# A six-deep pipeline of a vision tower: the order lists of four engines laid out anew

## What is computed

```python
h = _L0_tok_ref(x, L0_tok_W, L0_tok_b)
h = jnp.concatenate([jnp.broadcast_to(cls_tok, (h.shape[0], 1, h.shape[2])), h], axis=1)
h = h + _L0_attn_ref(_layernorm(h, axis=-1), ...)   # 12 heads of 64, diagonal out, top 12 of 17 kept, softmax, w_out
h = h + _L0_ffn_ref(_layernorm(h, axis=-1), ...)    # ternary weights, int8-like activations, silu(gate) * up
h = h + _L1_attn_ref(_layernorm(h, axis=-1), ...)   # causal linear attention, 12 heads of 16, gated by an "interference"
h = h + _L1_ffn_ref(_layernorm(h, axis=-1), ...)    # relu, two projections, layernorm
return h
```

## Time and profile before

| | us |
|---|---|
| median of 3 runs | 718.96 |
| the runs | 718.26, 719.4, 718.96 |
| the profiled execution, device time | 718.05 |
| its span, first to last instruction | 716.2 |
| PE busy | 596.5 (83%) |
| VectorE busy | 534.0 (75%) |
| GpSimd busy | 349.6 (49%) |
| ScalarE busy | 255.5 (36%) |

### The profile page before, as it was taken

One profiled execution on the slowest core, in us unless ns is written; L12 is line 12 of the kernel. 1 busy time (PEld: TensorE's weight loads), 2 busy tenths in 40 slices (PEclk: granted clock), 3 DMA queues, 4 the chain that ended last, 5 costly groups with the idle time before them and its releaser, 6 DMA issues.

```text
span 716.2 us, 15345 instructions
## 1 busy us (share of the span) xinstructions
PE 596.5 (83%) x5065; PEld 484.1 (68%) x5065; DVE 534.0 (75%) x2149; ACT 255.5 (36%) x659; POOL 349.6 (49%) x884
## 2 busy tenths in 40 slices
PE   4277878998999999899999998999998998778562
PEld 3165566776777777677777767777776777666451
DVE  0715568789888988889897898989889888864432
ACT  2014143443525344353533435353443534232110
POOL 2020023665645566564655656465655645454432
PEclk9679999999999999999999999999999999765555
DMA  9710010000000000000000000000000000000000
GB/s 220 166 35 1 1 41 19 2 20 6 22 9 18 26 7 21 7 19 20 9 19 5 19 5 19 17 11 21 5 0 5 1 6 7 0 6 0 6 1 7
DMA packets 11122, 14.92 MB, mean 21 GB/s; under 512 B 2161, under 2 KB 8658, under 8 KB 11078
## 3 DMA queue, kind: packets, MB, share of 16 engines
q1 hardware_dynamic: 8774, 12.69, 7.1%
q10 hardware_dynamic: 2304, 1.67, 0.8%
HBM read 12.68 MB, written 1.67 MB: 20 GB/s over the span
## 4 chain that ended last, share of the span: by engine, by line
PE 62%; DVE 15%; ACT 7%; POOL 6%; issue 5%; SPq 4%; DMA 1%; POOLq 0%; DVEq 0%; ACTq 0%
PE bank_embed L1211 8%; PE bank_lin L1346 5%; PE bank_embed L1216 5%; PE bank_embed L1181 4%; PE bank_lin L1368 4%; PE bank_embed L1195 4%; PE bank_att L1285 4%; PE bank_lin L1087 3%; PE bank_lin L1336 3%; PE bank_embed L1087 3%; SPq L387 3%; POOL rstd_h L483 3%; PE bank_lin L1384 2%; PE bank_att L1275 2%; PE bank_embed L1199 2%
## 5 line engine op out<-in xcount | busy, mean ns | idle before, releaser
L1211 PE MATMUL bank_embed<-norm0T,w_qkv 128*128 128x119 f32 x456 | 61.3, 287 | 11.4 <-DMA g_out<-L_ffn_g_out 6.5
L482 POOL TENSOR_TENSOR spread<-moments,gain_eps 119x1 f32<-119x1 f32 x57 | 10.9, 192 | 120.2 <-DVE moments L674 120.2
L1211 PEld LDWEIGHTS bank_embed<-norm0T,w_qkv 128*128 128x128 f32 x456 | 57.4, 202 | 12.4 <-issue 6.6
L483 POOL TENSOR_TENSOR rstd<-spread,minus_half 119x1 f32<-119x1 f32 (+1 forms) x95 | 55.5, 585 | 7.4
L530 POOL TENSOR_TENSOR feat_k<-feat_qk,consts 96x238 f32<-96x238 f32 x38 | 23.2, 627 | 73.3 <-DVE feat_qk L834 73.3
L984 ACT COPY qkT<-bank_embed 128x357 f32<-128x357 f32 x76 | 31.1, 467 | 50.0 <-PE bank_embed L1216 50.0
L1368 PE MATMUL bank_lin<-feat_qk,feat_k 32*119 32x119 f32 x456 | 46.1, 294 | 1.6 <-DVE weightsT L743 1.3
L699 DVE TENSOR_REDUCE scores<-bank_att 119x51 f32<-119x357 f32 x76 | 36.6, 522 | 14.3 <-PE bank_att L1245 13.2
L1368 PEld LDWEIGHTS bank_lin<-feat_qk,feat_k 32*119 32x119 f32 x456 | 38.6, 196 | 9.4 <-issue 5.2
L1181 PE MATMUL bank_embed<-w_tok,patchT 128*119 128x192 f32 x228 | 43.8, 344 | 0.9 <-ACT patchT L960 0.7
L483 POOL TENSOR_TENSOR rstd_h<-spread_h,minus_half 119x12 f32<-119x12 f32 x19 | 43.3, 2278 | 1.5
(11 more groups left out here) (232 smaller groups left out, 1602.1 us busy)
## 6 DMA issues: line engine op xcount, KB each, us to landing
strips<-x SPq DMA_DIRECT2D x19, 336.0 KB
out<-result ACTq DMA_DIRECT2D x18, 89.2 KB
w_qkv<-L_attn_w_qkv SPq DMA_DIRECT2D x2, 576.0 KB, 8.7
w_in_raw<-L_ffn_w_in SPq DMA_DIRECT2D x1, 768.0 KB, 11.7
w_tok_raw<-L_tok_W SPq DMA_DIRECT2D x1, 576.0 KB
w_qkv_rest<-L_attn_w_qkv SPq DMA_DIRECT2D x2, 288.0 KB, 9.1
w_o<-L_attn_w_out SPq DMA_DIRECT2D x1, 576.0 KB
w_qkv_raw<-L_attn_Wqkv SPq DMA_DIRECT2D x1, 432.0 KB
```

Source lines behind the costliest of these rows:

```text
L483: pool.tensor_tensor(rstd_out, spread, minus_half[0:ROWS, 0:spread.shape[1]], ALU.pow) \
L1211: pe.matmul(parts((E0, E1)[s], 3)[:, j], w_qkv0[:, tile * 128:(tile + 1) * 128], norm0T[:, s, :], start=j == 0, stop=False, skip_group_che ...
```

## The change

Only the four order lists change. No instruction is added, removed or altered; each engine runs the same steps in another order. Three steps get another number because they cross the end of the list: `t_lin_in` is now the first step of the next iteration (4 instead of 3), `v_mix` and `a_v` are the last ones of theirs (1 instead of 2, 0 instead of 1), `p_rstd3` and `v_norm3` the first ones (5 instead of 4). The number of iterations stays 24.

```diff
             iterations(pool, ...
-                (0, p_strips), (4, p_feat_k), (4, p_gate), (3, p_scaled), (3, p_rms), (5, p_rstd4),
-                (4, p_centred_sq), (4, p_rstd_h), (1, p_h0), (0, p_rstd0), (3, p_rstd2), (2, p_rstd1), (4, p_rstd3),
-                (4, p_h3_beta),
+                (5, p_rstd3), (0, p_strips), (1, p_h0), (4, p_feat_k), (4, p_gate), (3, p_scaled), (3, p_rms), (5, p_rstd4),
+                (4, p_centred_sq), (4, p_rstd_h), (3, p_rstd2), (0, p_rstd0), (2, p_rstd1), (4, p_h3_beta),
             iterations(dve, ...
-                (2, v_mix), (3, v_big_in), (4, v_hidT), (4, v_feat), (2, v_probs), (2, v_wide(0)), (2, v_wide(2)),
-                (5, v_stats4), (2, v_wide(1)), (4, v_causal[1]), (4, v_causal[0]), (3, v_gated), (4, v_causal[2]),
-                (4, v_v1), (3, v_big_out), (4, v_ratio), (5, v_result), (2, v_h1), (4, v_sq_sum), (2, v_u_in),
-                (1, v_pack(0, A0)), (1, v_pack(1, A1)), (4, v_att1), (0, v_h0), (0, v_stats0), (3, v_h2),
-                (3, v_stats2), (0, v_norm0), (1, v_pack(3, A1)), (1, v_pack(2, A0)), (3, v_norms2), (4, v_h3),
-                (1, v_top), (4, v_stats3), (1, v_drop), (4, v_norm3),
+                (5, v_norm3), (4, v_hidT), (3, v_big_in), (4, v_feat), (2, v_probs), (2, v_wide(0)), (2, v_wide(1)),
+                (2, v_wide(2)), (4, v_causal[0]), (5, v_stats4), (4, v_causal[1]), (3, v_gated), (4, v_causal[2]), (4, v_v1),
+                (3, v_big_out), (4, v_ratio), (5, v_result), (2, v_h1), (4, v_sq_sum), (2, v_u_in), (1, v_pack(1, A1)),
+                (3, v_h2), (1, v_pack(0, A0)), (3, v_stats2), (4, v_att1), (0, v_h0), (0, v_stats0), (3, v_norms2),
+                (1, v_pack(3, A1)), (0, v_norm0), (1, v_pack(2, A0)), (4, v_h3), (1, v_top), (1, v_drop), (4, v_stats3),
+                (1, v_mix),
             iterations(act, ...
-                (1, a_v(0)), (1, a_v(1)), (2, a_exp), (4, a_qk1), (5, a_norm3_T), (3, a_int_in), (5, a_hid1),
-                (4, a_tanh_par), (1, a_qk(0)), (3, a_in_T), (2, a_probsT[0]), (1, a_qk(1)), (3, a_tanh_gate),
-                (2, a_probsT[1]), (2, a_probsT[2]), (4, a_interference), (3, a_square), (4, a_num_T),
-                (2, a_att[0]), (2, a_att[1]), (3, a_int_out), (3, a_out_T), (5, a_store),
-                (0, a_patchT(1, E1, S["patches1"], S["patchT1"])), (0, a_patchT(0, E0, S["patches0"], S["patchT0"])),
-                (4, a_att1_T), (0, a_norm0T), (3, a_norms_T), (3, a_tanh_hid),
+                (4, a_qk1), (3, a_int_in), (2, a_exp), (5, a_norm3_T), (4, a_tanh_par), (1, a_qk(0)), (5, a_hid1),
+                (2, a_probsT[0]), (3, a_in_T), (2, a_probsT[1]), (3, a_tanh_gate), (2, a_probsT[2]), (4, a_interference),
+                (3, a_square), (2, a_att[0]), (1, a_qk(1)), (4, a_num_T), (2, a_att[1]), (3, a_int_out),
+                (0, a_patchT(0, E0, S["patches0"], S["patchT0"])), (3, a_out_T),
+                (0, a_patchT(1, E1, S["patches1"], S["patchT1"])), (5, a_store), (4, a_att1_T), (0, a_norm0T), (3, a_norms_T),
+                (0, a_v(0)), (0, a_v(1)), (3, a_tanh_hid),
             iterations(pe, ...
-                (5, t_norm3), (1, t_qk(0)), (4, t_params), (5, t_hid1), (3, t_int_in), (5, t_out4),
-                (4, t_lin((0, 1), S["a_done01"])), (2, t_probs(0)), (1, t_qk(1)), (3, t_gate), (2, t_probs(1)), (2, t_probs(2)),
-                (4, t_lin((2,), S["a_done2"])), (2, t_att0(0)), (4, t_num), (2, t_att0(1)),
-                (0, t_patches(1, E1, S["k_copied1"], S["patches1"])), (4, t_num_turn), (2, t_proj0),
-                (0, t_patches(0, E0, S["k_copied0"], S["patches0"])), (3, t_int_out), (1, t_dots(0)), (0, t_embed),
-                (3, t_down), (1, t_dots(1)), (4, t_att1), (0, t_norm0), (4, t_proj1), (0, t_v), (3, t_norms2),
-                (3, t_lin_in),
+                (4, t_lin_in), (5, t_norm3), (4, t_params), (1, t_qk(0)), (5, t_hid1), (4, t_lin((0, 1), S["a_done01"])),
+                (2, t_probs(0)), (3, t_int_in), (5, t_out4), (2, t_probs(1)), (2, t_probs(2)), (3, t_gate),
+                (4, t_lin((2,), S["a_done2"])), (1, t_qk(1)), (2, t_att0(0)), (2, t_att0(1)), (4, t_num),
+                (0, t_patches(0, E0, S["k_copied0"], S["patches0"])), (4, t_num_turn), (2, t_proj0),
+                (0, t_patches(1, E1, S["k_copied1"], S["patches1"])), (3, t_int_out), (1, t_dots(0)), (3, t_down),
+                (0, t_embed), (1, t_dots(1)), (4, t_att1), (4, t_proj1), (0, t_norm0), (3, t_norms2), (0, t_v),
```

## The result

The changed kernel takes **688.35 us** (687.62 to 690.81, 4 runs) against 719.18 (718.26 to 721.82, 4 runs): a ratio of 0.9572, 95% interval 0.9537 to 0.9606, or 30.8 us less. The forecast was 693.8, 25.2 less. The profiled execution of after took 690.81 with a span of 689.0; against 718.05 and 716.2 that is 27.2 less.

A forecast was written before the change was run, and what follows sets the result against it. PE was taken as the bound, with 27.6 us of own work a period. Order 19.6, fill 2.5 and clock 3.1 take 25.2 off 718.05, giving 692.9; the median, 0.9 above, is 693.8; range 684 to 708.

The forecast's parts named there:

- the main term: The new order in the 14 full periods: 1.4 us less waiting on PE in each, 19.6 us in all.
- since VectorE now reaches h1 just in time: PE's wait before dots(0), two short steps behind proj0: 0.1 to 0.25 us, taken as 0.1.
- rival 1: Norm3 on VectorE starts before GpSimd's strips' copy: period 29.0 us, all clock falls gone, 684 us; chance 0.14.
- The upper bound: H0's bias on GpSimd holds up big_in by 0.3 us, the gate chain and h1 by 0.3: period 30.2.
- rival 2: VectorE becomes the bound through its lock with GpSimd: period 30.2 us, time 702 to 705; chance 0.22.
- A is gone: PE's new wait of 0.6 us before norm3 vanishes if norm3 comes before the strips' copy: period 29.0.
- VectorE runs from v1 to h3 with under 0.1 to spare: VectorE's slack at ratio, h1 and h3: under 0.1 us, so any delay of VectorE there makes PE later.
- if they were gone it is the 0.57 again: PE's int_in wait goes because lin(0,1) and probs(0) cover hid1's copy; without them 0.57 us a period returns.
- Fill: First iterations: v's copies ahead of ScalarE's setup parts, and 1.1 us for thin iterations; 2.5 us less, bounds 0 and 4.
- none of it is reordered: 0: Last four iterations at 1.2 GHz, paced by one group's chain of dependences: no gain, bounds 2 us either way.
- Two of three falls away: Of three clock falls in the full periods, two vanish with the wait before num: 3.1 us, bounds 0 and 4.6.
- Rival 3: Slower: the clock falls twice in every full period, at PE's waits at num_turn and at proj1 with norms2: 734 us; chance 0.06.

## Why the prediction was right, and where not

**Where it came out.** 688.35 us lies inside the range that was given (684 to 708), but 0.65 below the band of the forecast itself (689 to 700). The gain in time was 30.8 us and not 25.2, while the period was longer than forecast, 29.94 and not 29.6. So the main term was too large and the others made up for it.

**The way of counting held.** PE's own work in a period was put at 27.6. By the same convention (a bracket and 0.16) after has these waits, each with its forecast in brackets: norm3 0.68 (0.6), num_turn 0.29 (0.35), dots(0) 0.26 (0.1), proj1 0.60 (0.6), norms2 0.49 (0.35), lin(0,1) 0.10 (none): 2.42 us (2.0). 29.94 - 2.42 = 27.5, and before gives 31.04 - 3.53 = 27.5. The prediction's own five terms for before (0.75, 0.80, 0.57, 1.16 and 0.25) add up to this 3.53, and not to the 3.4 that it wrote.

**The step that failed in the period** is the size of the small terms. 1.4 a period was forecast, 1.1 came. Dots(0) was put at 0.1 "since VectorE now reaches h1 just in time"; it is fixed by the chain from proj0 over h1, which takes 0.36 and two hand-overs, whatever VectorE did ahead of it. Norms2's hand-overs were 0.14 too short. Lin(0,1) was given none and starts 0.64 behind hid1. These three are 0.40 short; with norm3 (0.08 short) and num_turn (0.06 too long) the new waits are 0.42 longer than forecast. The slip in the old ones, 0.13, went the other way, so that the period missed by 0.3 only. Over 14 periods that is 4.2 of the 19.6 us.

**The lock.** That norm3 would lose to the copy was right (1.22; 1.1 was taken), and rival 1 did not occur: norm3 follows the last instruction of mix within 0.1 of the copy's start, and loses. The upper bound did not occur: amax_in takes 0.20 beside h0's bias, as it does without, so big_in was not held. What the bias can hold is mix (119x204), as the kernel with norm3 early showed. By its number alone the period (29.94) is nearer to rival 2 (30.2) than to the forecast, but the shorter gate chain gained nothing, and PE's waits account for the whole period: VectorE isn't the bound. "Below, A is gone, 0.6 a period less" is what the swap on GpSimd gave: 0.56. And att1 on VectorE takes 0.33 now, 0.74 before, since the bias is no longer beside it.

**"VectorE runs from v1 to h3 with under 0.1 to spare"** was wrong. With the longer gate chain VectorE came out of v1 0.3 later against PE than in after, and nothing behind it was late; with the chain shorter nothing was gained. V1 has 0.24 to spare before num, and the stretch behind it at least 0.3. The tight stretch of VectorE is another: h0 to hidT, as the kernel with att1 early showed.

**The gate.** The place of gate before q/k(1), claimed as what kept num waiting, is shown alone: 0.63 a period on the kernel before. Likewise int_in: "if they were gone it is the 0.57 again" (0.66). But that kernel loses 1.18 of the 1.10 that the whole change gains, so these gains don't add up; each is worth what it is only where the other gaps are closed.

**Fill.** 2.5 forecast (1.4 for the place of v's copies, 1.1 for thin iterations), 5.1 in the profile. The place of the copies is worth 1.3 to 3.2 of it, 1.9 at least came without it, and the rest can't be told apart with one profile of each kernel. The mechanism is shown in part, the size is not.

**Drain.** This step failed outright: "none of it is reordered: 0". The last iterations run the same new lists as the others. Those parts of the drain that have the same clock in both profiles took 29.57, 29.59 and 12.45 before and 28.82, 28.89 and 12.22 after, 1.7 us less; against that one iteration (30.33 and 30.57) gave 0.2 back. 1.0 of the 4.2 is only that norm0, the mark, now stands behind proj1. The other 1.8 are an iteration that has the clock at either level in both profiles, so that it isn't shown to belong to the lists.

**The clock.** "Two of three falls away" was one too few in this profile: 4.6 instead of 3.1. None of the twelve further profiles has a fall in the middle either, not even that with the old order and the gate first, nor that with 0.77 before num. The prediction placed the falls rightly: all three follow the wait of 1.00 before num. Why only every sixth of these waits is followed by one is open, and so is whether they come in every execution; the spread of before's times (717.9 to 727.49 in the first lot) is as large as several of them. Rival 3, slower through two falls a period, did not occur: the three waits of 0.33 to 0.52 in each period of after, and five of 0.32 to 0.51 in that of int_in's old place, left the clock at 2.4 GHz. The Trainium skill (TensorE: Matmul & The Clock Gate, "A second HAM failure mode: psum-queue depth-cycling") tells of another kernel, with bf16 matmuls of 512 columns, in which small pauses between groups of matmuls make the clock oscillate; no profile of the changed order shows this in the full periods.

**The sum.** Order 15.4 (19.6), fill 5.1 (2.5), clock 4.6 (3.1), drain 4.2 (0), start -2.2 (0): 27.2 against 25.2. Fill, clock and drain were too small by 2.6, 1.5 and 4.2, order and start too large by 4.2 and 2.2. That the total is off by 2.0 only is luck. The other 3.6 of the 30.8 are the profiled executions' distance from the medians: before's is 1.1 below its median, after's 2.5 above.

## What to carry over

Walk one period of the bounding engine with the old durations and write down each wait as bracket plus overlap: here that gave the new waits to 0.16 us each, and the sum to 0.4. Before a step is moved, ask what it covers where it stands now: int_in and out4 back in their old place cost 1.18 us a period, of which 0.48 was a gap that they had been filling. And where two engines share a lock, look for the long instruction of the one that meets a short one of the other on the critical path; a swap of two neighbours on GpSimd took 0.56 us off every period. Look, too, at the first step of each list in a hardware loop: here norm3 stood there, VectorE idled ahead of it at every turn, and the period with the turn was 0.12 us longer than the other in after and 0.6 in one variant.

## What the runs showed of the hardware

- Which instructions the lock held. Instructions of VectorE that lost to one of GpSimd: norm3 1.22 beside the copy of 1.03 and 0.65 beside the bias of 0.61 (0.38 alone), mix 0.76 beside the bias (0.34 alone), v1 0.85 beside `scaled`. The 119x1 operation amax_in took 0.20 beside the bias, as without it.
- Two profiles of kernels whose lists up to the first norm0 are the same differ by 2.6 us there (23.62 and 26.21), and two with nearly the same lists by 3.7 us in one iteration of the drain through the granted clock. A change of 5 us can't be read from two profiles' totals; the norm0 marks of the full periods agree to 0.12 us in 419 (419.17, 419.27, 419.24, 419.29 in four profiles with the same PE order).
- At each turn of the hardware loop VectorE sat idle ahead of the first step of its list: 0.15 to 0.19 us in after, 0.54 to 0.58 in the four kernels with norm3 right behind its statistics. In the full iterations before the first turn it was 0 to 0.23.
